# Re-tiling the token FFN of a fused vision and text block: six tiles of a pair become five, and the four engine lists are laid out again

## The reference

```python
h = concat([cls, tokenizer(x)], 1)            # two patch branches, five depthwise convs, LayerNorm
h = concat([h, txt], 1)                        # (32, 325, 192)
h = h + LayerNorm((q @ k.T * mask) @ v)        # q, k, v: two-layer MLPs of LayerNorm(h); mask: the 64 keys up to i
# the FFN, token by token (BitNet style)
xn = rmsnorm(LayerNorm(h)) * g_in
u, g = split(round(xn * 127 / max|xn|) @ ternary(w_in).T)      # 192 -> 2 x 512
y = rmsnorm(silu(g) * u) * g_out
out = h + round(y * 127 / max|y|) @ ternary(w_out).T           # 512 -> 192
```

## Time and profile before

| | before |
|---|---|
| median of three runs | 1199.82 us (1197.52 to 1203.08) |
| span of the profiled execution, first to last instruction | 1195.4 us |
| PE busy | 1081.3 us, 90% |
| DVE busy | 1033.5 us, 86% |
| ACT busy | 963.3 us, 81% |
| POOL busy | 812.7 us, 68% |
| FFN tiles (count of L1394) | 96 |

### The profile page before, as it was taken

The page is one execution under the profiler, slowest core; times in us unless marked ns, Lnnn a source line. Parts: engine busy times, 40 slices in busy tenths (PEclk is TensorE's granted clock), DMA queues, the critical chain, the costliest instruction groups (busy, mean ns, idle before and its releaser), DMA issues.

```text
span 1195.4 us, 19559 instructions
## 1 busy us (share of the span) xinstructions
PE 1081.3 (90%) x5674; PEld 736.5 (62%) x5674; DVE 1033.5 (86%) x3013; ACT 963.3 (81%) x2437; POOL 812.7 (68%) x860
## 2 busy tenths in 40 slices
PE   6877999999999999999999999999999897878544
PEld 3655676767676767677676757676766655545311
DVE  1887598999999999999999999999999997856653
ACT  4656687899989898989999988989898978766543
POOL 4446486868687777878686868787786857562521
PEclk9898999999999999999999999999999998979655
DMA  8101010101010100101010101001010000000000
GB/s 327 62 27 41 8 41 7 50 7 57 9 57 9 46 17 16 49 13 50 13 53 7 56 9 54 9 16 50 16 47 15 10 11 15 10 15 9 9 12 14
DMA packets 21513, 40.25 MB, mean 34 GB/s; under 512 B 2656, under 2 KB 18208, under 8 KB 19104
## 3 DMA queue, kind: packets, MB, share of 16 engines
q1 hardware_dynamic: 21408, 39.01, 9.4%
HBM read 31.02 MB, written 7.99 MB: 33 GB/s over the span
## 4 chain that ended last, share of the span: by engine, by line
PE 76%; DVE 9%; ACT 7%; issue 4%; POOL 2%; DMA 1%; SPq 0%; POOLq 0%; DVEq 0%; ACTq 0%
PE bank L398 14%; PE bank L517 7%; PE bank L428 7%; PE bank L439 4%; PE bank L430 4%; PE bank L438 4%; PE bank L376 4%; PE bank L377 3%; PE bank L539 3%; PE bank L458 3%; PE bank L459 3%; DVE bank L1214 2%; PE bank L471 2%; PE bank L472 2%; PE bank L587 2%
## 5 line engine op out<-in xcount | busy, mean ns | idle before, releaser
L1214 DVE SCALAR_TENSOR_TENSOR bank<-padA,c_col,bank 128x406 f32<-128x406 f32 x560 | 357.9, 639 | 7.6
L398 PE MATMUL bank<-x_sb,w_emb 128*128 128x392 f32 x576 | 216.6, 507 | 6.5 <-ACT padA L755 3.7
L810 ACT ACTIVATE prod<-padB,c_col 128x196 f32<-128x196 f32 x432 | 174.3, 449 | 5.1 <-POOL accB L1734 2.5
L1703 POOL TENSOR_TENSOR yg<-y_f,c_gout 128x512 f32<-128x512 f32 (+1 forms) x96 | 122.6, 1278 | 45.9 <-DVE y_f L1404 45.8
L398 PEld LDWEIGHTS bank<-x_sb,w_emb 128*128 128x128 f32 x576 | 102.3, 192 | 60.8 <-ACT padA L755 5.6
L810 ACT ACTIVATE early<-padB,c_col 128x196 f32<-128x196 f32 x288 | 120.7, 449 | 2.3 <-POOL accB L1734 2.2
L517 PE MATMUL bank<-w_in,xq 128*128 128x512 bf16 (+1 forms) x384 | 109.1, 411 | 13.6 <-ACT xq L873 13.6
L1696 POOL TENSOR_TENSOR s<-s,c_mhalf 128x1 f32<-128x1 f32 (+1 forms) x96 | 55.2, 575 | 90.8 <-ACT s L886 90.8
L867 ACT ACTIVATE yq<-bank 128x512 bf16<-128x512 f16 (+1 forms) x96 | 50.2, 523 | 50.8 <-PE bank L529 50.8
L879 ACT ACTIVATE th<-bank,sm 128x512 f32<-128x512 f32 (+1 forms) x96 | 65.3, 681 | 31.6 <-PE bank L517 31.1
L1385 DVE SCALAR_TENSOR_TENSOR ya<-th,bank 128x512 f32<-128x512 f32 (+1 forms) x96 | 65.1, 678 | 26.5 <-ACT th L879 26.3
(11 more groups left out here) (219 smaller groups left out, 3229.3 us busy)
## 6 DMA issues: line engine op xcount, KB each, us to landing
x_sb<-xt SPq DMA_DIRECT2D x16, 1176.0 KB, 5.3
out<-o_sb SPq DMA_DIRECT2D x64, 96.0 KB
w_sq<-squares SPq DMA_DIRECT2D x1, 3840.0 KB, 15.6
h_sb<-txt SPq DMA_DIRECT2D x32, 51.8 KB
out<-o_sb SPq DMA_DIRECT2D x32, 51.8 KB
h_sb<-txt SPq DMA_DIRECT2D x32, 44.2 KB
w_in<-win SPq DMA_DIRECT2D x1, 1024.0 KB, 17.6
c_row<-broads SPq DMA_DIRECT2D x1, 672.0 KB, 19.2
```

Of the source, the lines that this page charges most:

```text
L398: done = mm(pE[:, 0:2 * N_PATCH], w_emb[:, k, m, :], x_sb[:, k, :], start=k == 0, stop=k == KC - 1)
L810: made = go(grid(prod[ACC[s] ^ 1][:, k, :]), tap_view(padB[min(s, 2)], SIDE, k), ACT.Copy, scale=tapcol(s, 1, k))
L1214: v.scalar_tensor_tensor(grid(acc if k == TAPS - 1 else run), tap_view(pad, ROWS_A, k), tapcol(s, 0, k), grid(run), ALU.mult, ALU.add).the ...
L1703: g.tensor_tensor(yg[0:m, :], y_f[0:m, :], c_gout[0:m, :], ALU.mult).then_inc(f_yg, 1)
```

## The change

- **Tiles.** `NF` = 5 tiles of a pair, all with 128 rows: the two full tiles of each image, and one tile (number 2) that holds 64 rows of each image's last tile. The five rows that are left over in each image are copied into a buffer `left`. A sixth tile runs over that buffer for only two pairs (`LEFT`): pair 11, with the 120 rows of pairs 0 to 11, and pair 15, with the 40 rows of pairs 12 to 15.
- **Copies.** A new step `join` on SP waits for h2 of the pair, copies the two sets of five rows into `left`, waits for these copies (`taken`), and then copies 64 rows of the second image into rows 64 to 127 of tile 2 (`joined`). `hidden_bn` waits for `joined` ahead of tile 2, which it now takes last. `output_add` waits for the join of the pair that used its h2 buffer before.
- **Stores.** Tile 2 is stored by two DMAs. The sixth tile is stored by one DMA for each image, 24 for pair 11 and 8 for pair 15.
- **Lists.** All five lists (PE, ACT, DVE, POOL, SP) are in a new order. The turn's edges are cut elsewhere, so a pair counts eight stages (`DEPTH` 7 to 8) and there are 23 turns, the first of which holds next to nothing.
- The two `sm` buffers are cleared at the start.

The diff, cut to its core; of the lists, the stretches that the prediction speaks of:

```diff
+NF = NT - 1
+SPARE = ROWS[2] - SPAN
+LEFT = (11, PAIRS - 1)
-DEPTH = 7
+DEPTH = 8
+def tiles_of(f):
+    return NF + (f in LEFT)
+def tile_no(f, n):
+    return f * NF + sum(x < f for x in LEFT) + n
+def left_rows(f):
+    return 2 * SPARE * (f - (LEFT[0] if f > LEFT[0] else -1))
+def rows_of(f, n):
+    return P if n < NF else left_rows(f)
...
+        left = [sb(f"left{i}", [P, D]) for i in range(2)]
...
+        def joint(f, par, n):
+            return h2[par][:, n, :] if n < NF else left[f > LEFT[0]][0:left_rows(f), :]
...
             def store(f, n):
+                if n == NF:
+                    for i in range(left_rows(f) // SPARE):
+                        image = 2 * f + 2 - left_rows(f) // SPARE + i
+                        sp.dma_start(out[image, T - SPARE:T, :],
+                                     o_sb[at][i * SPARE:(i + 1) * SPARE, :]).then_inc(stored[at], 16)
+                elif n == 2:
+                    for img in range(2):
+                        sp.dma_start(out[f * 2 + img, 2 * P:T - SPARE, :],
+                                     o_sb[at][img * SPAN:(img + 1) * SPAN, :]).then_inc(stored[at], 16)
...
+            def join(f, par):
+                sp.wait_ge(h2_ready, f + 1)
+                lo = left_rows(f) - 2 * SPARE
+                for img in range(2):
+                    sp.dma_start(left[f > LEFT[0]][lo + img * SPARE:lo + (img + 1) * SPARE, :],
+                                 h2[par][SPAN:ROWS[2], 2 + img * TILES, :]).then_inc(taken, 16)
+                sp.wait_ge(taken, (f + 1) * 32)
+                sp.dma_start(h2[par][SPAN:P, 2, :], h2[par][0:SPAN, 2 + TILES, :]).then_inc(joined, 16)
...
             # SP, one turn
+                if on[6]: store(it - 6, 2); store(it - 6, 3); store(*last_tile(it - 6))
+                if on[3]: load_txt(it - 3); load_cls(it - 3)
+                if on[0]: load_x(it)
+                if on[5]: store(it - 5, 0)
+                if on[4]: join(it - 4, par)
+                if on[5]: store(it - 5, 1)
...
             def hidden_bn(f, par, tiles):
                 for n in tiles:
-                    m = ROWS[n % TILES]
-                    done = v.bn_stats(st_f[0:m, n, :], h2[par][0:m, n, :])
+                    if n == 2:
+                        dve.wait_ge(joined, (f + 1) * 16)
+                    done = v.bn_stats(st_f[:, n, :], h2[par][:, n, :])
...
             # DVE, from output_stats to the first tile (conditions left out)
+                output_stats(it - 5); taps(it - 2, G_, 7); taps(it - 2, G_, 8); finished(it - 6, 1)
+                taps(it - 3, F2_, 0..8) with hidden_round(0..4, it - 6, 2), gated(it - 6, 3) among them
+                lifted(it - 6, 3); taps(it - 2, L_, 0..3); hidden_bn(it - 5, odd, (0, 1, 3))
+                finished(it - 6, 2); taps(it - 2, L_, 4..6) with hidden_round(0..4, it - 6, 3) among them
+                hidden_bn(it - 5, odd, (4, 2)); taps(it - 2, L_, 7); gated(it - 6, 4)
+                token_scale_0(it - 5, odd); lifted(it - 6, 4); token_gain(it - 5, odd, ...)
+                taps(it - 2, L_, 8); token_scale_1(it - 5, odd); token_scale_2(it - 5, odd)
+                add_loc(it - 3); hidden_round(0, it - 6, 4); hidden_round(1, it - 6, 4)
+                taps(it - 3, F3_, 0); finished(it - 6, 3); hidden_round(2, it - 6, 4)
+                taps(it - 3, F3_, 1); hidden_round(3 and 4, it - 6, 4); token_scale_3(it - 5, odd)
...
             # POOL
XX(it - 4, par)
-                    hidden_scale(it - 5, 4); hidden_root(it - 5, 4); second_root(it - 4, par)
-                    hidden_root(it - 5, 5); hidden_scale(it - 5, 5)
+               first_root(it - 5, odd); hidden_scale(it - 6, 4); hidden_root(it - 6, 4)
+               second_root(it - 5, odd); biased_tokens(it - 4)
+               if it - 6 in LEFT: hidden_scale(it - 6, 5); hidden_root(it - 6, 5)
...
             # PE, the seam between two turns
+                mlp_half(it - 4, 'qw2', U_Q2, hq)
+                rounded_token_transposes(it - 5, 0)
+                embed_chunk(it - 1, EMB_GA, range(0, 2))
+            # next turn
+                ffn_in(it - 6, 0)
+                mlp_wide(it - 5, 'kw2', U_K2, hk)
```

More of the change, by code:

```diff
@@ L346, in turn @@
                 if on[5]:
+                    store(it - 5, 0)
+                if on[4]:
+                    join(it - 4, par)
+                if on[5]:
                     store(it - 5, 1)
[L348 to L354 removed]
             for dst, src in EARLY:
@@ new lines, in turn @@
+                if on[4]:
+                    layer_F3(it - 4, 1)
+                if on[7]:
+                    ffn_out(*last_tile(it - 7))
+                if on[5]:
+                    mlp_half(it - 5, 'kw2', U_K2, hk)
+                if on[6]:
+                    rounded_token_transposes(it - 6, 1)
+                if on[5]:
+                    values(it - 5, 0)
+                if on[6]:
+                    ffn_in(it - 6, 1)
+                if on[2]:
+                    embed_chunk(it - 2, EMB_GA, range(2, 4))
@@ new lines, in turn @@
+                if on[6]:
+                    rounded_token_transposes(it - 6, 2)
+                if on[2]:
+                    embed_chunk(it - 2, EMB_LA, range(0, 2))
+                if on[6]:
+                    ffn_in(it - 6, 2)
+                if on[5]:
+                    mixed_values(it - 5, 0)
+                    mixed_values(it - 5, 1)
+                    mixed_values(it - 5, 2)
+                if on[2]:
+                    embed_chunk(it - 2, EMB_LA, range(2, 4))
+                if on[3]:
+                    layer_F1(it - 3)
@@ new lines, in turn @@
+                if on[6]:
+                    rounded_token_transposes(it - 6, 3)
+                if on[4]:
+                    mlp_wide(it - 4, 'qw1', U_Q1, xT)
+                if on[6]:
+                    ffn_in(it - 6, 3)
+                if on[2]:
+                    layer_W2(it - 2)
+                if on[4]:
+                    mlp_half(it - 4, 'qw1', U_Q1, xT)
+                if on[6]:
+                    rounded_hidden_transposes(it - 6, 2)
+                if on[1]:
+                    embed_chunk(it - 1, EMB_BB, range(0, 2))
@@ new lines, in turn @@
+                if on[6]:
+                    ffn_out(it - 6, 2)
+                if on[4]:
+                    mlp_wide(it - 4, 'kw1', U_K1, xT)
+                if on[2]:
+                    if first(it - 2):
+                        weight_totals()
+                if on[6]:
+                    rounded_token_transposes(it - 6, 4)
+                if on[1]:
+                    embed_chunk(it - 1, EMB_BB, range(2, 4))
+                if on[6]:
+                    ffn_in(it - 6, 4)
+                if on[1]:
+                    embed_chunk(it - 1, EMB_BB, range(4, 6))
@@ L1652, in turn @@
[L1652 to L1665 removed]
+                if on[6]:
+                    hidden_round(4, it - 6, 1, par)
+                    gated(it - 6, 2)
@@ new lines, in turn @@
+                if on[2]:
+                    taps(it - 2, L_, 7)
+                if on[6]:
+                    gated(it - 6, 4)
+                if on[5]:
+                    token_scale_0(it - 5, odd)
+                if on[6]:
+                    lifted(it - 6, 4)
+                if on[5]:
+                    token_gain(it - 5, odd, range(0, 3))
+                    token_gain(it - 5, odd, range(3, NF))
+                if on[2]:
+                    taps(it - 2, L_, 8)
+                if on[5]:
+                    token_scale_1(it - 5, odd)
+                    token_scale_2(it - 5, odd)
@@ new lines, in turn @@
+                if on[3]:
+                    taps(it - 3, F3_, 1)
+                if on[6]:
+                    hidden_round(3, it - 6, 4, par)
+                    hidden_round(4, it - 6, 4, par)
+                if on[5]:
+                    token_scale_3(it - 5, odd)
+                if on[3]:
+                    taps(it - 3, F3_, 2)
+                if on[6]:
+                    if it - 6 in LEFT:
+                        gated(it - 6, 5)
+                    if it - 6 in LEFT:
+                        lifted(it - 6, 5)
@@ new lines, in turn @@
+                if on[3]:
+                    taps(it - 3, F3_, 5)
+                    taps(it - 3, F3_, 6)
+                    taps(it - 3, F3_, 7)
+                    taps(it - 3, F3_, 8)
+                if on[2]:
+                    mix(it - 2)
+                if on[5]:
+                    gated(it - 5, 0)
+                    lifted(it - 5, 0)
+                if on[2]:
+                    taps(it - 2, F1_, 0)
+                if on[3]:
+                    token_biased(it - 3, 0)
@@ new lines, in turn @@
+                if on[4]:
+                    values_out(it - 4, 0)
+                if on[5]:
+                    hidden_round(2, it - 5, 0, odd)
+                if on[2]:
+                    taps(it - 2, F1_, 3)
+                if on[5]:
+                    hidden_round(3, it - 5, 0, odd)
```

(7 more changed lines are left out.)

1236 lines of the change are left out of this document (565 added, 671 removed).

## The result

The changed kernel takes 1191.1 us (median of four runs, 1190.7 to 1191.3), the kernel before 1199.8; the ratio is 0.9931, with a 95% interval from 0.9912 to 0.9949. It is faster, by some 8 us, where 21 were forecast. (In the diff ahead of the prediction, the line of POOL's list that reads `XX(it - 4, par)` stands for `biased_tokens(it - 3); first_root(it - 4, par)`.)

A forecast was written before the change was run, and what follows sets the result against it. PE was taken to bound the even turns, DVE next, and order and latency the drain. Span 1195.4 - 12 (turns) - 11 (drain) + 2 (last store) = 1174.4 us, plus 4.4 gives 1178.8, called 1179; range 1160 to 1200.

The forecast's parts named there:

- The even turns: Eleven full-pipeline turns, bound by PE: 1.1 us less each, 12 us in all, bounds 0 and 18.
- floor of 63.20: PE's work in a new even turn: 64.45 us less 1.25 us, for two small tiles replaced by one full.
- The fill: Start of the program: same sequence of layers over the pairs in both lists, costed at nothing, within 3 us either way.
- The drain: After the last new embedding: pairs 12, 13 and 14 lose a tile each, 11 us less, bounds 4 and 27.
- the sum of 11 us: Drain gain from lost tiles: 5 us each for pairs 12 and 13, 1.2 for pair 14; bounds 4 and 27.
- the six more of pair 15: Last pair's final store becomes eight DMAs of about 0.37 us issue each instead of one: 2 us more.
- The lock: Rival, chance 0.12: POOL's biased_tokens blocks DVE near token_scale_3; if in every turn, 21 us more, time 1200.
- The stores: Pair 11's 24 stores hold SP about 9 us ahead of load_txt; costed at nothing, 2 us if cover is short.
- Pair 11's sixth tile: Pair 11 keeps six tiles in the DVE-bound stretch from 927 us, so that stretch stays as it was.
- The join and the seam: Even turns: join's two hops, 3.1 us, hidden at no cost; rival seam, chance 0.10: late join stalls PE, time 1217.
- The 4.4 us between span and median: Added to the forecast span of 1174.4 us, as the median of the runs lies that far above the span.

The follow-up runs named there:

- the other mends: Against the changed kernel: first pair's old ACT order, and last pair's biased_tokens ahead of first_root; 1181.0 us, or 1176.7 us with pair 11's stores also moved.

## Why the prediction was wrong, point by point

- **The even turns: right, with a term too small.** Forecast a gain of 1.1 us a turn; measured 1.27, with no wait of DVE for a DMA in these turns. PE sets the turn, as said. But PE's work fell by 64.45 - 62.78 = 1.67 us and not by 1.25, below the floor of 63.20, and 0.4 of that was lost to idle time. The two errors nearly cancel, so the nearness of 1.1 and 1.27 is in part luck. That order and tile pull against each other (+2.3, -3.6) did not show in the sum.
- **The fill: the failed step is "the sequence of layers over the pairs is the same in both lists; I cost it at nothing".** The sequence of layers was compared, but not each engine's order in the turns of the first pair. Two instructions of ACT stood behind waits that only a full pipeline covers: 7 us; some 0.9 more stand ahead of the first embedding (15.15 against 14.23) and were not followed.
- **The drain: the failed step is the sum of 11 us, not the tiles' worth.** Three tiles are worth some 15 us (15.1 by the medians, 15.3 and 17.2 by the profiles; forecast 11, bounds 4 and 27). The step counted what was removed and held the new order to be free there. By the single profiles it cost 6.4 us by the lists, and 9.2 by the stores as read at six tiles; the six more of pair 15, forecast at 2 us, are 2.0 of these. The lock and the clock behind it are worth some 4 us in the changed kernel (3.6 by the ratios, 4.9 by the medians). The step as a whole is shown by the run with six tiles and the new lists; where the lists' 5.2 us ahead of h2 of pair 14 arise stays open.
- **The stores: mis-sized.** "Nothing, 2 us if that cover is short": the 24 stores did take 8.06 us (forecast 9), the cover was short by 4.7, and moving them gave back 2 us alone and 4.3 beside the other mends, which the intervals do not tell apart.
- **Pair 11's sixth tile:** taken as unchanged; its turn grew by 1.5 us.
- **The lock: mechanism and instruction right, how often it strikes wrong.** It struck in one pair of sixteen, 2.35 us, and some 2 us again by the clock, not in eleven turns. The first step of `token_scale_3` reads two SBUF operands and ended with POOL's instruction (1080.62 + 2.50 = 1083.12, 1080.48 + 2.63 = 1083.11). The Trainium skill ("SBUF — State Buffer", Who interferes with whom) says that a DVE instruction with two SBUF inputs contends with a GpSimd instruction that reads SBUF, and this row agrees. L1332, which the prediction calls to witness, reads one SBUF operand (mv_f), so the rule of two inputs does not cover it; no run here shows what held it.
- **The join and the seam:** cost nothing, as forecast, but by luck. The two hops took 4.5 us and not 3.1 (I had allowed 5), the cover was 0.9 us, and beyond it and some 0.8 us of idle time each microsecond is one of the turn.
- **The 4.4 us between span and median:** it was not a constant. The profiled execution of after is 1.9 us above its span. The executions of the kernel before spread from 1197.5 to 1203.1 us, and a span of 1195.4 belongs to the lower end. So the spans differ by 6.1 us where the medians differ by 8.7.

In sum: -14.9 - 1.0 + 8.0 + 1.5 + 0.3 = -6.1 us of span, against -21.

## What to carry to other kernels

When the lists of a software pipeline are laid anew, walk each engine's list three times: with all stages full, with the first item alone, and with the last ones alone. An order that costs nothing when the pipeline is full may cost its whole wait at either end. Price a removed piece of work and the new order that comes with it as two terms; here they were of the same size, with opposite signs, and a kernel that has the new order and the old work measures the second. An engine that is idle for 3 us of a turn may have far less slack than that (here 0.8 us) if the wait lies in the chain that feeds the bounding engine.

## What the runs showed of the hardware

A wait of 2.4 us on PE cost more than itself: the granted clock fell to a mean of 0.73 over the 10 us around it, four matmuls took 2.37 us in place of 1.29, and with eight idle matmuls in the wait (1.89 us) the clock stayed at 1.00 and the stretch behind the wait took 4.37 us in place of 6.24. In the last pair, where PE stands more than it works, idle matmuls took the clock from 0.50 to 0.96 and a tile's step from 7.75 to 6.27 us.
